# Preparing the binary and ternary weights inside expert layer 0 instead of ahead of it

## The reference

```
x = x + 0.5 * L0_ffn(layernorm(x));  x = x + L0_attn(layernorm(x));  x = x + 0.5 * L0_ffn(layernorm(x))
x = x + 0.5 * L1_ffn(layernorm(x));  ...
x = x + 0.5 * L2_ffn(layernorm(x));  ...   # weights W_fc, W_proj made ternary
x = x + 0.5 * L3_ffn(layernorm(x));  ...   # weights w1, w2 made binary
```

```
ternary (absmean): gamma = mean(|W|) + 1e-6;  Wq = sign(W) * min(round(|W| / gamma), 1)
binary:            alpha = mean(|w|, axis=1); bw = alpha * sign(w);  w + (bw - w)
```

## Time and profile before

| | |
|---|---|
| time, median of 3 runs | 2892.66 us (2884.6 to 2895.79) |
| the profiled execution, its own time | 2887.91 us |
| its span in the profile | 2886.2 us |
| mean granted TensorE clock in it | 0.949 |
| PE busy | 2623.6 us, 91% of the span |
| DVE busy | 2288.4 us, 79% |
| ACT busy | 1873.5 us, 65% |
| POOL busy | 526.2 us, 18% |

### The profile page before, as it was taken

How to read it: one execution, slowest core, us unless ns; L and a number is a source line. 1 busy time by engine, 2 the same in 40 slices (tenths; PEclk the granted TensorE clock), 3 DMA queues, 4 the chain that set the end, 5 groups by cost and what they waited for, 6 DMA issues and landing times. The chain is left out here.

```text
span 2886.2 us, 50752 instructions
## 1 busy us (share of the span) xinstructions
PE 2623.6 (91%) x19244; PEld 982.7 (34%) x19244; DVE 2288.4 (79%) x3516; ACT 1873.5 (65%) x3735; POOL 526.2 (18%) x847
## 2 busy tenths in 40 slices
PE   5998989899999999889978999999999799978778
PEld 2436634222222222623322222222227333245336
DVE  5456545799999998587868999999984887855993
ACT  2212322599999999556655999999995567655103
POOL 0000000200111110122312110111102232223761
PEclk9997999699999999989996999999999899989989
DMA  3220122400000000221114000000000311010000
GB/s 121 85 68 1 42 82 58 147 20 20 19 21 21 21 22 27 62 82 53 41 32 143 21 20 21 19 21 20 21 27 14 108 42 53 26 31 30 0 0 16
DMA packets 71996, 120.80 MB, mean 42 GB/s; under 512 B 16905, under 2 KB 44041, under 8 KB 68586
## 3 DMA queue, kind: packets, MB, share of 16 engines
q1 hardware_dynamic: 71754, 117.57, 12.7%
HBM read 94.19 MB, written 23.33 MB: 41 GB/s over the span
## 5 line engine op out<-in xcount | busy, mean ns | idle before, releaser
L1247 ACT ACTIVATE arena<-ps 128x512 f32<-128x512 f32 (+3 forms) x2816 | 1427.2, 570 | 267.0 <-PE ps L1052 242.1
L1375 DVE TENSOR_REDUCE arena<-ps 128x1 f32<-128x1024 f32 x1024 | 1172.2, 1214 | 22.5 <-PE ps L954 20.7
L954 PE MATMUL ps<-arena 61*128 61x512 bf16 (+4 forms) x2816 | 851.8, 380 | 42.5 <-DVE arena L1375 21.0
L1052 PE MATMUL ps<-arena 64*128 64x512 bf16 (+4 forms) x2816 | 837.0, 371 | 41.4 <-ACT arena L1247 19.8
L981 PE MATMUL ps<-arena 128*32 128x256 f32 (+2 forms) x9200 | 806.5, 422 | 0.4 <-POOL arena L1332 0.4
L1377 DVE CUSTOM_DVE_ANT_0 ps<-ps,arena 128x896 f32<-128x896 f32 (+7 forms) x512 | 376.2, 784 | 83.5 <-PE ps L954 79.6
L1052 PEld LDWEIGHTS ps<-arena 64*128 64x128 bf16 (+1 forms) x2816 | 184.6, 95 | 704.3 <-ACT arena L1247 564.2
L981 PEld LDWEIGHTS ps<-arena 128*32 128x32 f32 x9200 | 181.3, 108 | 422.3 <-ACT arena L1247 211.1
L954 PEld LDWEIGHTS ps<-arena 61*128 61x128 bf16 (+1 forms) x2816 | 192.3, 96 | 166.0 <-DVE arena L1375 84.3
L347 PE MATMUL ps<-xnT,moe_up 128*128 128x512 f32 x448 | 214.9, 605 | 0.0
L1301 POOL TENSOR_TENSOR arena<-arena,ones 16x128 bf16<-16x128 f32 x96 | 43.2, 450 | 902.6 <-ACT arena L1232 847.5
(11 more groups left out here) (244 smaller groups left out, 2510.9 us busy)
## 6 DMA issues: line engine op xcount, KB each, us to landing
arena<-m_w SPq DMA_DIRECT2D x40, 256.0 KB, 3.0
arena<-f_q SPq DMA_DIRECT2D x60, 144.0 KB
arena<-f_k SPq DMA_DIRECT2D x180, 48.0 KB
arena<-in_w SPq DMA_DIRECT2D x4, 2048.0 KB
arena<-a_q SPq DMA_DIRECT2D x14, 576.0 KB
arena<-a_k SPq DMA_DIRECT2D x42, 192.0 KB
a_q<-arena SPq DMA_DIRECT2D x44, 96.0 KB, 2.0
a_k<-arena SPq DMA_DIRECT2D x44, 96.0 KB, 2.0
```

Of the source, the lines that this page charges most:

```text
L954: last = nc.tensor.matmul(at[:, k0 // CHUNK, 0:n], score_rows(Qop[par], j, slice(q0, q0 + P)), score_rows(Kop[par], j, slice(k0, k0 + n)), ...
L1052: nc.tensor.matmul(ps[:, ring_bank(item), off:CHUNK], shifted_rows(Kop[par], j, slice(kb * P, (kb + 1) * P)), shifted_rows(Qop[par], j, sl ...
L1247: nc.scalar.activation(pr[:, (at % 2) * 4 + j, off:CHUNK], ps[:, ring_bank(item), off:CHUNK], ACT.Exp).then_inc(s.ex, 1)
L1375: nc.vector.tensor_reduce(top, src, AXX, ALU.max).then_inc(s.sread, 1)
```

## The change

1. Boot keeps the loads, the normalisation of the first 512 tokens and two small casts. Its mean and variance wait for x alone (a new semaphore, xin); the casts wait for the five small loads.
2. SP starts moe_gate, moe_up and moe_dn ahead of the four raw matrices, which increment a new semaphore, raw_weights.
3. The quantisation goes into expert layer 0 (`quantise=True` for m0 alone), cut into pieces that stand in DVE's list between `gated(n)` and `weigh(n-9)` of steps 14, 18, 24, 26, 28, 31, 34, 41, 43, 45 and 47. PE's three sums stand in steps 22, 30 and 38 between `up(n)` and `down(n-10)`, in a PSUM bank (GATE) that the layer no longer uses by then. ACT's two signs stand in steps 16 and 18.
4. The raw matrices and their scratch move to the end of the arena, which layer 0 does not use.

SP's list, before and then after. The names are the tensor written and the one read; `in_` is an input of the kernel.

The core of the diff:

```diff
-        def moe(tag, after):
+        cw = Carve()
+        cw.at = RAW_AT = ARENA - 6 * FF - 8
+        raw_fc, raw_pj, raw_a, raw_b = (cw(FF) for _ in range(4))
+        tmp_v, tmp_s = cw(FF), cw(FF)
+        gam = cw(8)
+        RAW_LOADS = (("fc2", raw_fc), ("pj2", raw_pj), ("w13", raw_a), ("w23", raw_b))
+
+        def moe(tag, after, quantise=False):
...
+                def sum_ternary():
+                    pe.wait_ge(s.wcopy, CHUNKS)
+                    pe.wait_ge(s.gabs, 1)
+                    nc.tensor.matmul(ps[:, GATE, 0:2], ones[:, :], gam[:, 0:2], start=True, stop=True)\
+                        .then_inc(s.gsum, 1)
+
+                def sum_up():
+                    pe.wait_ge(s.gabs, 2)
+                    nc.tensor.matmul(ps[:, GATE, :], ones[:, :], tmp_v, start=True, stop=True)\
+                        .then_inc(s.gsum, 1)
+
+                def sum_down():
+                    pe.wait_ge(s.gabs, 3)
+                    for f in range(FT):
+                        last = nc.tensor.matmul(ps[:, GATE, 0:D], ones[:, :], tmp_v[:, f * D:(f + 1) * D],
+                                                start=f == 0, stop=f == FT - 1)
+                    last.then_inc(s.gsum, 1)
...
+                    if quantise and n == 22:
+                        sum_ternary()
+                    if quantise and n == 30:
+                        sum_up()
+                    if quantise and n == 38:
+                        sum_down()
                     m = n - LAG
                     if m >= 0:
                         down(m)
...
+                    if quantise and n == 16:
+                        act.wait_ge(raw_sem, 16 * len(RAW_LOADS))
+                        nc.scalar.activation(w3a[:, :], raw_a, ACT.Sign).then_inc(s.bsign, 1)
+                    if quantise and n == 18:
+                        nc.scalar.activation(w3b.rearrange("p f d -> p (f d)"), raw_b, ACT.Sign)\
+                            .then_inc(s.bsign, 1)
...
+                def magnitudes(k, src, dst):
+                    t.settle(dve, nc.vector.scalar_tensor_tensor(dst, src, -1.0, src, ALU.mult, ALU.max))
+                    return nc.vector.tensor_reduce(gam[:, k:k + 1], dst, AXX, ALU.add)
...
+                def ternarise(k, src, dst):
+                    t.settle(dve, nc.vector.tensor_scalar(tmp_s, src, gam[:, 4 + k:5 + k], None, ALU.is_lt))
+                    t.settle(dve, nc.vector.scalar_tensor_tensor(dst, src, gam[:, 2 + k:3 + k], tmp_s,
+                                                                 ALU.is_gt, ALU.subtract))
...
+                def quantised(n):
+                    if n == 14:
+                        dve.wait_ge(raw_sem, 16 * len(RAW_LOADS))
+                        t.settle(dve, magnitudes(0, raw_fc, tmp_s))
+                    if n == 18:
+                        magnitudes(1, raw_pj, tmp_v).then_inc(s.gabs, 1)
+                    if n == 24:
+                        thresholds()
+                    if n == 26:
+                        nc.vector.scalar_tensor_tensor(tmp_v, raw_a, -1.0, raw_a, ALU.mult, ALU.max)\
+                            .then_inc(s.gabs, 1)
+                    if n == 28:
+                        ternarise(0, raw_fc, w2fc[:, :])
+                    if n == 31:
+                        ternarise(1, raw_pj, w2pj.rearrange("p f d -> p (f d)"))
+                    if n == 34:
+                        dve.wait_ge(s.gsum, 2)
+                        dve.wait_ge(s.bsign, 2)
+                        binarise(w3a[:, :], ps[:, GATE, :], raw_a, 1.0 / D)
+                        nc.vector.scalar_tensor_tensor(tmp_v, raw_b, -1.0, raw_b, ALU.mult, ALU.max)\
+                            .then_inc(s.gabs, 1)
+                    if n in (41, 43, 45, 47):
+                        f = (n - 41) // 2
+                        dve.wait_ge(s.gsum, 3)
+                        binarise(w3b[:, f, :], ps[:, GATE, 0:D], raw_b[:, f * D:(f + 1) * D], 1.0 / FF)
...
+                    if quantise:
+                        quantised(n)
                     m = n - LAG + 1
                     if m >= 0:
                         weigh(m)
...
         def boot_sync(sp):
...
+            sp.dma_start(x, a["x"]).then_inc(boot.xin, 16)
+            for dst, name in BOOT_LOADS:
                 sp.dma_start(dst, a[name]).then_inc(boot.const, 16)
             for dst, name in ((moe_gate, "gate0"), (moe_up, "up0"), (moe_dn, "down0")):
                 sp.dma_start(dst, a[name]).then_inc(moe_sem, 16)
-        NBOOT = 160
+            for name, dst in RAW_LOADS:
+                sp.dma_start(dst, a[name]).then_inc(raw_sem, 16)
...
-        def boot_tensor(pe):
...
-        def boot_scalar(act):
...
         def boot_vector(dve):
             t = Tally(boot.vec)
-            dve.wait_ge(boot.const, NBOOT)
             nc.vector.memset(neghalf[:, :], -0.5).then_inc(boot.bw, 1)
+            nc.vector.memset(ones[:, :], 1.0)
+            dve.wait_ge(boot.xin, 16)
             ahead_stats(dve, boot, t, 0, "single")
...
-            (moe, ("m0",)),
+            (moe, ("m0", True)),
```

More of the change, by code:

```diff
@@ L309, in moe @@
             wts = c(TILES * 9).rearrange("p (n e) -> p n e", e=9)
+            assert c.at <= RAW_AT
             wd = dram(f"{tag}_w", [CHUNKS, 9, CHUNK])
-            s = sems(tag, "stats rstd xn tp xT vec pool gmm gcopy gtp shift gexp wts wtp wcopy ws "
+            s = sems(tag, "gabs gsum bsign stats rstd xn tp xT vec pool gmm gcopy gtp shift gexp wts wtp wcopy ws "
                           "wl0 wl1 wl2 wl3 wl4 up silu raw hw dn ycopy y x")
@@ L549, in add, with thresholds @@
                     nc.vector.tensor_tensor(x[:, r], x[:, r], ps[:, TP, :], ALU.add).then_inc(s.x, 1)
+                def magnitudes(k, src, dst):
+                    t.settle(dve, nc.vector.scalar_tensor_tensor(dst, src, -1.0, src, ALU.mult, ALU.max))
+                    return nc.vector.tensor_reduce(gam[:, k:k + 1], dst, AXX, ALU.add)
+                def thresholds():
+                    dve.wait_ge(s.gsum, 1)
+                    t.settle(dve, nc.vector.tensor_scalar(gam[:, 2:4], ps[:, GATE, 0:2], 1.0 / (D * FF), 1e-6,
+                                                          ALU.mult, ALU.add))
+                    t.settle(dve, nc.vector.tensor_scalar(gam[:, 2:4], gam[:, 2:4], 0.5, None, ALU.mult))
+                    t.settle(dve, nc.vector.tensor_scalar(gam[:, 4:6], gam[:, 2:4], -1.0, None, ALU.mult))
@@ L2444, in lion @@
             return dict(tensor=tensor, scalar=scalar, gpsimd=gpsimd, vector=vector, sems=s)
-        cw = Carve()
-        raw_fc, raw_pj, raw_a, raw_b = (cw(FF) for _ in range(4))
-        tmp_v, tmp_s = cw(FF), cw(FF)
-        gam = cw(8)
+        BOOT_LOADS = ((ident, "ident"), (masks, "masks"), (lower, "lower"), (cols[:, 0:n_cols - 4], "cols"),
+                      (rows[0:1, :], "rows"))
         def boot_sync(sp):
-            for dst, name in ((x, "x"), (ident, "ident"), (masks, "masks"), (lower, "lower"),
-                              (cols[:, 0:n_cols - 4], "cols"), (rows[0:1, :], "rows"), (raw_fc, "fc2"),
-                              (raw_pj, "pj2"), (raw_a, "w13"), (raw_b, "w23")):
+            sp.dma_start(x, a["x"]).then_inc(boot.xin, 16)
+            for dst, name in BOOT_LOADS:
                 sp.dma_start(dst, a[name]).then_inc(boot.const, 16)
@@ L2465, in boot_gpsimd @@
             rstd_gpsimd(pool, boot, Tally(boot.pool), 0)
-        def boot_tensor(pe):
-            pe.wait_ge(boot.gabs, 1)
-            nc.tensor.matmul(ps[:, 0, 0:2], ones[:, :], gam[:, 0:2], start=True, stop=True)\
-                .then_inc(boot.gsum, 1)
-            pe.wait_ge(boot.gabs, 2)
-            nc.tensor.matmul(ps[:, 1, :], ones[:, :], tmp_v, start=True, stop=True)\
-                .then_inc(boot.gsum, 1)
-            pe.wait_ge(boot.gabs, 3)
-            for f in range(FT):
-                last = nc.tensor.matmul(ps[:, 2, 0:D], ones[:, :], tmp_v[:, f * D:(f + 1) * D],
-                                        start=f == 0, stop=f == FT - 1)
-            last.then_inc(boot.gsum, 1)
-        def boot_scalar(act):
-            act.wait_ge(boot.const, NBOOT)
-            nc.scalar.activation(w3a[:, :], raw_a, ACT.Sign).then_inc(boot.bsign, 1)
-            nc.scalar.activation(w3b.rearrange("p f d -> p (f d)"), raw_b, ACT.Sign)\
-                .then_inc(boot.bsign, 1)
         def boot_vector(dve):
             t = Tally(boot.vec)
-            dve.wait_ge(boot.const, NBOOT)
             nc.vector.memset(neghalf[:, :], -0.5).then_inc(boot.bw, 1)
+            nc.vector.memset(ones[:, :], 1.0)
+            dve.wait_ge(boot.xin, 16)
             ahead_stats(dve, boot, t, 0, "single")
-            nc.vector.memset(ones[:, :], 1.0)
+            dve.wait_ge(boot.const, 16 * len(BOOT_LOADS))
             nc.vector.tensor_copy(identb[:, :], ident[:, :])
@@ L2578, in run @@
             nc.all_engine_barrier()
-        run(dict(sync=boot_sync, tensor=boot_tensor, scalar=boot_scalar, vector=boot_vector,
```

(2 more changed lines are left out.)

38 lines of the change are left out of this document (6 added, 32 removed).

## The result

| | median us | lowest to highest | executions |
|---|---|---|---|
| before, beside it | 2889.21 | 2884.60 to 2895.79 | 4 |
| after | 2866.28 | 2864.43 to 2872.91 | 4 |

The ratio is 0.9928, with an interval of 0.9904 to 0.9953: faster by 22.9 us, 0.7%. The forecast was 2877 in a range of 2864 to 2889, with 13.7 us gained. The profiled execution of after took 2872.91 us with a span of 2871.2, which is 15.0 less than the 2887.91 and 2886.2 of before. So one execution with a trace stands close to the forecast's sum and the medians do not; where the other 8 us come from was the question for the experiments.

A forecast was written before the change was run, and what follows sets the result against it. PE, busy 91% of the span, bounds the kernel: 19.3 us gained at the head, less 3.9 of stops and 1.7 of sums, gives 13.7. Between 2874.2 profiled and 2879 median it gave 2877, range 2864 to 2889.

The forecast's parts named there:

- The head: Start of the program: the gate's product would start at 14.5 instead of 33.77, 19.3 us gained (18.6 to 20.5).
- The race: In the head, the norm (13.3) and the expert weights (seen 14.4 to 14.6) race to the gate's product; weights end later.
- The norm's chain: In the head: x seen at 6.2, the norm's last step from 9.4 to 10.5, gate's product possible at 13.3.
- The raw loads: Land by 17.3, step 14 at 67, wait costs nothing; rival that they slow the weights: 2880, chance 0.10.
- The stops: Layer 0's steps: DVE pieces longer than the room ahead of `weigh` stop PE, 3.9 us in all (2.2 to 7.6).
- The room of 0.98: Layer 0's steps: a piece between `gated` and `weigh` stops PE only by its excess over 0.98 us, plus 0.10.
- both other readings: Room as DVE's whole idle time, 1.28 us (stops 2.2), or up to the weight load, 0.60 us (stops 7.6).
- PE's sums: Layer 0: three added sums on PE, 0.86, 0.9 and 0.3, less 0.4 back in step 38: 1.7 us (1.2 to 2.2).
- Layer 0 longer by 5.6: From the gate's product to layer 0's end, 5.6 us longer, from stops of 3.9 and PE's sums of 1.7.
- The clock at 1.0: PE's granted clock stays at 1.0 from step 14 to the end of layer 0.
- The fourth case: Rival: new stops drop PE to half clock inside layer 0, 2.58 us more per step, 2903 for ten; chance 0.06.
- Net 13.7: Whole kernel: 19.3 less 3.9 less 1.7 gives 13.7 us gained (8.8 to 17.1), profiled execution 2874.2.

The follow-up runs named there:

- xonly: Kernel before, with DVE's first wait for x alone and the quantisation still in boot: 2885.03 us, one execution.
- rawfirst: Changed kernel with the four raw loads issued ahead of the expert weights again: 2868.67 us, ratio 0.9939 to the kernel before.
- noq: Changed kernel without any quantisation, raw matrices loaded straight into the weight tiles: 2864.24 us, ratio 0.9919 to the kernel before.
- spread: Changed kernel with the same quantisation cut to one settled instruction per step of layer 0: 2863.02 us, ratio 0.9917 to the kernel before; repeated at 2867.76.
- again: Changed kernel unaltered, timed again beside the kernel before: 2869.02 us, ratio 0.9943.
- again2: Changed kernel unaltered, timed a third time beside the kernel before: 2871.86 us, ratio 0.9948.
- spread_gate: As spread, but the gate's first product waits for its own load only: 2866.24 us, ratio 0.9929 to the kernel before; repeated at 2865.35.
- warm: As spread_gate, with 32 unused products of a ones matrix on PE during boot: 2861.49 us, ratio 0.9917 to the kernel before.

## Why the prediction was right, point by point

- **The head, 19.3 forecast (18.6 to 20.5): 20.3.** The race and its winner were right. Mis-sized was when the weights are seen: 13.4 instead of 14.4. 305 GB/s up to 9.67 are 2.95 MB instead of 2.70, so the 4.14 MB were through at 9.67 + 1.19 / 0.386 = 12.75, 0.6 earlier than reckoned; and they were seen 0.65 behind the last byte, not 1.0. x too was seen 0.6 behind its bytes (5.80, forecast 6.2). Both numbers hang on the order of the issues, which the forecast took over from before: the ten traces with the weights ahead have 305 to 311 GB/s up to 9.67, the three with the raw loads ahead 279, 288 and 294 (before, xonly, rawfirst). In rawfirst the weights are again seen about 1.0 behind their last byte (15.65 by the same count, 16.64). Why the order changes them is open.
- **The norm's chain: L204 ends at 10.5; it ended at 9.78**, since x came 0.4 earlier and POOL took 1.04 instead of 1.32. It set nothing.
- **The raw loads cost nothing: right.** Nothing in step 14 waits for them. That order holds is shown by rawfirst.
- **The stops, 3.9 forecast (2.2 to 7.6): 4.2.** One by one: step 14 0.57 (0.56), step 18 0.44 (0.44), steps 28 and 31 0.43 each (0.42), step 34 1.90 (1.88), and steps 41 to 47 0.10 each, the exposed load alone, for 0.05. The room of 0.98 from the earlier trace rows was right and both other readings wrong. (By its own pieces the upper bound comes to 7.7, not 7.6.)
- **PE's sums, 1.7 forecast (1.2 to 2.2): 1.43** by noq and spread. The ternary sum took 0.22 of new time, not 0.3; the credit of 0.42 for the load that is no longer exposed came as written; one by one the rows make 0.22 + 0.86 + 0.89 - 0.42 = 1.55.
- **Layer 0 longer by 5.6: 5.65** between the marks. From L385 to its end, as the forecast had it, it is 5.8 in this trace and 6.4 and 7.6 in again and again2, since the stretch ahead of the first mark, put at no change, took 0.1, 0.7 and 1.9 more than in before.
- **Table load at the start of layer 0: not in the forecast.** The forecast took the 1.89 us from L278 to L376 over from before. They held (1.90 in spread_gate), but in after the load ends only 0.02 us ahead of PE's turning.
- **The clock at 1.0 from step 14 to the layer's end: right.** The fourth case, half clock inside layer 0, is refuted: 135.39 and 135.40 in five traces.
- **Net 13.7 of the profiled execution (2874.2): 15.0 (2872.91)**, of which 1.0 is the head, 0.4 lies behind layer 0, and the smaller sums, the larger stops and the first 46 us of the layer take 0.1 together. The given 2877 split the way between the profiled execution and a median of three (2892.66) that lay 6 us over what 39 executions of before show (2886.4). Taken from that level the sum gives 2872.7, and the sixteen executions of the kernel have 2869.5.

The step that carried no number was the scatter of the comparison itself: I said that 14.5 us can be told from no change, and with four executions each the gain came out 8 us too large. The range held it, by 2.3 us, and owes that to the 7 us it allowed for the clock. So the mechanism and the sum were right, and that the first median came out inside was in part luck.

## What to carry to other kernels

Work at the head of a program that one engine does alone is paid in full; put into a loop of another engine's steady steps it costs only what each piece is longer than the room ahead of the instruction that the bounding engine waits for. Read that room as the distance from the feeding instruction's end to the start of its consumer, less what the take-up needs (here 87.55 to 88.58 less 0.05, 0.98 us), not as the feeding engine's idle time (1.28), and cut the pieces to single instructions that fit. Where a difference of under 1% is to be judged, compare marks inside the traces and times at equal mean clock, since medians of four to six executions were off by up to 8 us.

## What the runs showed of the hardware

- Mean granted clock, with one program: 0.947 to 0.954. By the fit that goes with 12 us in 2886, 0.30 us for each us at half clock.
- PE idle ahead of layer 0 (6.0 us in before, 10.7 in after) ran its first products at little over half of the later speed: 1.86 to 1.88 for the gate's two in twelve traces, 1.02 where 64 idle instructions ran ahead (warm). There the granted clock fell to 0.50 at 15.5 to 16.0 all the same, behind waits of 0.90, 1.19 and 0.68 us. When the speed rises varied: to the third turning it took between 46.3 and 48.6 us with the same instructions, and 45.65 in warm.
- A product that waits 0.31 us takes 1.12 instead of 1.02, with its weight load exposed; a piece that ends just at the room's edge costs that 0.10 without any wait shown.
- By the count of bytes, loads were seen 0.6 us behind their last byte in after (x at 5.80, moe_dn at 13.4), 1.0 to 1.2 in before, 1.0 in rawfirst and 1.6 in xonly (the ten loads through at 2.43 / 0.288 = 8.4, seen at 10.02): not one constant. 1.05 MB put ahead of a load moved it by 3.2 us. The Trainium skill (DMA: Bandwidth & Descriptors, "Queues, rings and completion order") has each DMA engine taking its descriptors in ring order; rawfirst agrees with that.
- ACT's signs inside layer 0 (71.39 and 76.54) brought no table load: the trace has none around them. A table load took 1.28 us, and at the start of layer 0 the copy behind it began 0.01 to 0.06 us after its end (after, spread_gate, warm).
